# Ternary group means: ScalarE scales the sums out of PSUM into bfloat16, VectorE only applies the lower bound

## The reference

```python
def ternary_quant(w_fp32, g=64):
    w = w_fp32.astype(jnp.bfloat16)
    w_g = w.reshape(-1, g)
    scale = jnp.clip(jnp.mean(jnp.abs(w_g), axis=-1, keepdims=True), 1e-08, None)
    q = jnp.clip(jnp.round(w_g / scale), -1, 1)
    w_hat = (q * scale).reshape(w.shape)
    return w + jax.lax.stop_gradient(w_hat - w)
```

## Time and profile before

| | us |
|---|---|
| median of 3 runs | 684.52 |
| lowest and highest | 682.62, 688.56 |
| the profiled execution | 689.13 |
| its span, first to last instruction | 687.2 |
| TensorE busy | 569.5 |
| VectorE busy | 490.9 |
| ScalarE busy | 307.2 |
| GpSimd busy | 216.8 |

### The profile page before, as it was taken

One profiled execution on the slowest core, in us unless ns is written; L12 is line 12 of the kernel. 1 busy time (PEld: TensorE's weight loads), 2 busy tenths in 40 slices (PEclk: granted clock), 3 DMA queues, 4 the chain that ended last, 5 costly groups with the idle time before them and its releaser, 6 DMA issues.

```text
span 687.2 us, 10946 instructions
## 1 busy us (share of the span) xinstructions
PE 569.5 (83%) x3678; PEld 405.9 (59%) x3678; DVE 490.9 (71%) x1066; ACT 307.2 (45%) x563; POOL 216.8 (32%) x225
## 2 busy tenths in 40 slices
PE   2777699689577799998599988898978889999990
PEld 1544377468356688884355554464535478888870
DVE  5799966997895486868558678768871467777753
ACT  2749222223322233551456545545535656666640
POOL 2666556247544223674200010010044011121120
PEclk9999899899699899996789999999979999999995
DMA  6222000000320005499954331500025793000005
GB/s 183 85 82 88 1 0 1 1 0 17 87 63 16 1 1 174 90 207 259 199 89 80 71 70 26 95 2 2 2 76 231 277 372 123 23 24 32 24 31 191
DMA packets 32733, 58.36 MB, mean 85 GB/s; under 512 B 6822, under 2 KB 24646, under 8 KB 30118
## 3 DMA queue, kind: packets, MB, share of 16 engines
q1 hardware_dynamic: 30422, 52.32, 28.4%
q0 software_dynamic: 1872, 5.13, 2.1%
q10 hardware_dynamic: 384, 0.20, 0.1%
HBM read 41.84 MB, written 15.51 MB: 83 GB/s over the span
## 4 chain that ended last, share of the span: by engine, by line
PE 39%; DVE 9%; DMA 4%; ACT 3%; POOL 2%; issue 2%; SPq 1%; ACTq 0%; POOLq 0%; DVEq 0%
PE bank L826 19%; PE bank L1089 5%; PE bank L820 4%; PE bank L1066 4%; DVE small L1828 3%; PE bank L1039 3%; DMA Qs<-mT 2%; PE bank L1068 1%; PE bank L1041 1%; DMA pieces<-P 1%; SPq L721 1%; ACT PTa L1372 1%; DMA yt<-results 1%; PE bank L1106 1%; POOL P3c L2258 1%
## 5 line engine op out<-in xcount | busy, mean ns | idle before, releaser
L1828 DVE TENSOR_REDUCE small<-bank 128x1 f32<-128x256 f32 (+3 forms) x256 | 107.7, 483 | 15.1 <-PE bank L1041 14.1
L1039 PE MATMUL bank<-Ks,Qs 96*128 96x256 bf16 (+3 forms) x256 | 66.6, 328 | 8.5 <-DVE small L1828 7.1
L2094 DVE TENSOR_TENSOR wl<-wall,wh 128x1024 fp32r<-128x1024 f32 x46 | 56.2, 1222 | 22.2 <-ACT wh L1511 20.9
L1066 PE MATMUL bank<-Qs,Ks 99*128 99x512 bf16 (+3 forms) x256 | 60.4, 312 | 7.9 <-DMA Qs<-mT 5.6
L1372 ACT ACTIVATE PTb<-bank 128x512 f32<-128x512 f32 (+1 forms) x96 | 43.9, 529 | 34.9 <-PE bank L1068 34.4
L1372 ACT ACTIVATE PTa<-bank 128x512 f32<-128x512 f32 (+1 forms) x96 | 43.5, 529 | 33.8 <-PE bank L1068 28.9
L1066 PEld LDWEIGHTS bank<-Qs,Ks 99*128 99x128 bf16 x256 | 25.6, 100 | 51.4 <-issue 24.5
L1041 PE MATMUL bank<-maskb,identb 128*128 128x128 bf16 x256 | 55.3, 234 | 0.0
L1323 ACT ACTIVATE sg<-bank 128x512 f32<-128x512 f32 (+1 forms) x28 | 16.7, 598 | 75.9 <-PE bank L826 75.9
L1511 ACT CAST wh<-wall 128x1024 fp32r x46 | 48.0, 1044 | 1.8 <-issue 0.7
L1068 PE MATMUL bank<-identb,maskb 128*128 128x128 bf16 x256 | 48.2, 225 | 0.0
(11 more groups left out here) (362 smaller groups left out, 1531.2 us busy)
## 6 DMA issues: line engine op xcount, KB each, us to landing
wall<-e_pack SPq DMA_DIRECT2D x8, 1536.0 KB, 8.4
Qs<-pieces SPq DMA_DIRECT2D x48, 128.0 KB, 6.0
stg<-w_pack SPq DMA_DIRECT2D x18, 256.0 KB, 2.7
pieces<-P SPq DMA_DIRECT2D x9, 512.0 KB, 9.9
wf<-t_pack SPq DMA_DIRECT2D x12, 256.0 KB, 2.7
Ks<-pieces SPq DMA_DIRECT2D x8, 384.0 KB, 5.5
sorted_rows<-blank SPq DMA_DIRECT2D x1, 2944.0 KB, 12.1
Ks<-pieces SPq DMA_DIRECT2D x8, 256.0 KB, 5.7
```

What stands on the lines that cost most here:

```text
L1039: nc.tensor.matmul(banks[b][:, o:o + w], Q[0:96, h, i * P:(i + 1) * P], K[0:96, h, 0:w], start=True, stop=False)
L1066: nc.tensor.matmul(banks[b][:, o:o + w], K[0:99, h, j * P:(j + 1) * P], Q[0:99, h, j * P:CH], start=True, stop=False)
L1828: last = nc.vector.tensor_reduce(mxv[:, i, h:h + 1], banks[b][:, o:o + w], AX.X, ALU.max, negate=True)
L2094: nc.vector.tensor_tensor(weight_part("l", i, half), wall[:, bass.ds(place + half * KC * EI, KC * EI)], weight_part("h", i, half).bitcast( ...
```

## The change

The mean is split in two. A new function `group_mean` on ScalarE copies the sums from bank 3 with the scale 1/64 into `scl` (bfloat16), once per piece, and takes over the two waits for the former contents of `scl`. VectorE then applies only the lower bound, from `scl` to `scl` in SBUF ("the bound"), and waits for ScalarE instead of TensorE. TensorE may write bank 3 again when ScalarE has read it. Nothing else is moved; the new ScalarE instruction stands where the sums stand in the table of slots.

```diff
--- before.py
+++ after.py
@@ -326,6 +326,7 @@
         decay = tally("decay_ready")
         sgl = tally("silu_g_ready")
         t_abs = tally("ternary_abs")
+        t_mean = tally("ternary_mean")
         t_scl = tally("ternary_scale")
         t_sgn = tally("ternary_digits")
         t_over = tally("ternary_difference")
@@ -890,7 +891,7 @@
                 ab, scl, over = L0["ab"][:, i % 4, :], L0["scl"][:, i % 2, :], L0["over"][:, i % 2, :]
                 same_group, minus_half = L0["grp"][:, 0, :], L0["grp"][:, 1, :]
                 b = TERN_BANKS[stage]
-                claim(b, (t_scl, t_sgn, t_put)[stage], p)
+                claim(b, (t_mean, t_sgn, t_put)[stage], p)
                 if stage == 0:
                     pe.wait_ge(*t_abs.upto((p, 0)))
                     pe.wait_ge(*setup.upto("grp"))
@@ -1314,6 +1315,14 @@
                 nc.scalar.activation(L0["ab"][:, i % 4, :], L0["wf"][:, i % 2, :], ACT.Abs).then_inc(*t_abs.tick((p, 0)))
                 nc.scalar.activation(L0["sgn"][:, i % 4, :], L0["wf"][:, i % 2, :], ACT.Sign).then_inc(*t_abs.tick((p, 1)))
 
+            def group_mean(p):
+                i = PIECES.index(p)
+                act.wait_ge(*mm.upto(("tern", p, 0)))
+                if i >= 2:
+                    act.wait_ge(*t_over.upto(PIECES[i - 2]))
+                    act.wait_ge(*mm.upto(("tern", PIECES[i - 2], 1)))
+                nc.scalar.activation(L0["scl"][:, i % 2, :], banks[TERN_BANKS[0]][:], ACT.Copy, scale=1.0 / 64).then_inc(*t_mean.tick(p))
+
             def mlp_gate(s, gb):
                 (kind, c), m, n = steps[s]
                 M = SW[m] if kind == "sw" else P
@@ -1412,6 +1421,8 @@
                     nc.scalar.activation(v, v, ACT.Silu).then_inc(*sgl.tick((c, pr)))
                 elif op == "ternA":
                     absolute(it[1])
+                elif op == "tern" and it[2] == 0:
+                    group_mean(it[1])
                 elif op == "w" and it[1] in ("w1", "w3", "w2"):
 
                     if it[1] == "w2":
@@ -1635,13 +1646,12 @@
                 i = PIECES.index(p)
                 bank = banks[TERN_BANKS[stage]]
                 scl, digit = L0["scl"][:, i % 2, :], L0["tern"][:, i % 2, :]
+                if stage == 0:
+                    dve.wait_ge(*t_mean.upto(p))
+                    nc.vector.tensor_scalar(scl, scl, 1e-8, None, ALU.max).then_inc(*t_scl.tick(p))
+                    return
                 dve.wait_ge(*mm.upto(("tern", p, stage)))
-                if stage == 0:
-                    if i >= 2:
-                        dve.wait_ge(*t_over.upto(PIECES[i - 2]))
-                        dve.wait_ge(*mm.upto(("tern", PIECES[i - 2], 1)))
-                    nc.vector.tensor_scalar(scl, bank[:], 1.0 / 64, 1e-8, ALU.mult, ALU.max).then_inc(*t_scl.tick(p))
-                elif stage == 1:
+                if stage == 1:
                     dve.wait_ge(*t_abs.upto((p, 1)))
                     nc.vector.scalar_tensor_tensor(digit, bank[:], 0.0, L0["sgn"][:, i % 4, :], ALU.is_gt, ALU.mult)\
                         .then_inc(*t_sgn.tick(p))
```

## The result

The kernel after takes 695.05 us (median of 4 runs, 692.11 to 696.55), the kernel before 686.54 us (median of 4, 682.62 to 689.99; three of the four are the runs that the prediction stood on). The ratio is 1.0122 with a 95% interval of 1.0075 to 1.0170, which is 8.4 us longer (5.1 to 11.7). The forecast was 690.1 us, with 694.0 as the upper end. So the direction was right and the size too small. A loss of more than 1% had a chance of 0.28 in the prediction, and this is one.

The account below looks back on a forecast made before the run. The prediction took VectorE's repeating slot of work per weight piece to bound the kernel. Start 2.6, regular slots 2.5 and long slots 0.5 gave +5.6 us, on the median 684.52 a forecast of 690.1 us, range 685.0 to 694.0.

Parts of the forecast that it names:

- What bounds the kernel: Ternary weight stage, 30 to 87 us: whatever starts VectorE's next slot later, one slot per weight piece, makes the kernel longer.
- The start: First pieces: the first mean copy queues on ScalarE behind signs that wait for a DMA; +2.6 us, bounds 2.3 and 2.9.
- The longer way: Third piece at the start: sums, copy, bound take 0.87 us to VectorE's next instruction against 0.64 before, so 0.23.
- the clock: Rival, TensorE at the start and in slots: its clock stays low after the longer pause; +7.4, 691.9 us; chance 0.06.
- The price of the bound: VectorE's bound in SBUF takes 0.30 us instead of 0.69; 0.39 saved 12 times, 4.7 us the whole possible gain.
- What takes the gain: Seven regular slots: GpSimd's read-out holds the bound, which ends 0.15 us behind it; slots of 4.41 us, +2.5 us.
- The long slots: Two slots with the value rows: ScalarE's decay rows get behind the copy; bounds 0 and 1.0, taken as +0.5 us.
- (1): Rival, regular slots: the bound passes beside GpSimd unheld; the start remains, +2.3, 686.8 us; chance 0.20.
- (2): Rival, VectorE: its relief decides, all 4.7 us come through against the start's 2.6; -2.1, 682.4 us; chance 0.06.
- (3): Rival, VectorE's bound: it stays at one element a cycle, 0.39 more in seven slots; +8.3, 692.8 us; chance 0.10.
- (4): Rival, TensorE: its clock stays low after the longer pause, with products and sums slower; +7.4, 691.9 us; chance 0.06.

Follow-up runs that it names:

- e3: The whole change, but on ScalarE the first piece's mean copy stands ahead of the third piece's absolute values and signs; ratio 1.0034 to the kernel before.
- e7: The whole change, but in the first long slot ScalarE does decay rows, then mean copy, then values and signs; ratio 1.0110 to the kernel before.
- e4: The whole change, but the bound is a three-operand instruction that also reads the sums from PSUM; ratio 1.0118 to the kernel before.
- e5: The whole change, but ScalarE's copy adds 1e-8 as a bias and VectorE applies no bound; ratio 0.9971 to the kernel before.
- e9: The whole change with a bound also reading PSUM, and the first piece's copy ahead of the third's values and signs; ratio 1.0059 to the kernel before.

## Why the prediction was right and wrong

**What bounds the kernel: right.** What starts VectorE's next slot later made the kernel longer: the interval of each ratio holds the shift of the last split. That the two spans differ by 7.2 us as the last splits do (7.19) is partly luck, as what lies behind the last split scatters by 6.6 us.

**The start: the cause right, the size not, 3.54 instead of 2.6.** The queue behind the DMA was named, and e3, which changes only the place in it, takes the whole loss away. Three things were left out of the term. The first bound ended 2.66 late instead of 2.33, as the DMA came 0.22 later and the copy did not overlap the signs; the 0.22 belongs to this execution, and e7, whose start is the same, has 3.21 in all. The longer way was counted at the third piece only; the second piece paid 0.31 too. And the clock, which stood among the rivals at 0.06, was part of it: TensorE's pause was 5.05 us instead of 2.48, the granted clock in the start's stretch (30 to 42.4 us) 0.59 against 0.80 before (30 to 38.5), and products and sums took 1.43 instead of 1.17 us, 0.26 more. That the longer pause made the clock low was not tested. 2.66 + 0.31 + 0.26, and 0.31 for the third piece (0.23 forecast), are the 3.54. The bound of 2.9 on this term was too tight: it took a held bound as the only thing that could go wrong.

**The price of the bound: right.** 0.293 us free, 0.30 forecast.

**What takes the gain: right.** Slots of 4.42 to 4.45 against 4.41, +2.66 against +2.5. e4 shows the hold as what makes all seven slots alike, and e5 what a slot is without the bound. The averages agree, but not slot by slot: the slots of before take 3.51 to 4.38, and in the one of 3.51 some 0.5 of the loss of 0.94 would be there without a hold, by the longer way (e4, e9). What of the bound needs something that GpSimd holds, its reading, its writing or its form, was not taken apart.

**The long slots: 0.98 instead of 0.5.** The step considered only the decay rows behind the copy and took the middle of its bounds. It did not ask whether the bounds of the long slots are held as well. In the first (+0.60) the wait for the copy made the loss after the change, and in e7, without that wait, the hold made the same; the hold makes the second (+0.38).

**Rivals.** (1), the bound passing beside GpSimd, is out: in all seven regular slots it ended 0.15 or 0.16 us behind the read-out. (2) is out, as VectorE's busy time shows no relief. (3) is out, 0.29 us where GpSimd is idle. (4) did not decide, but it put 0.26 into the start; in the slots the read-out covered it, as the prediction said (0.95 of cover; the slot at a clock of 0.69 took 4.42).

**The range.** What failed is the size of two terms of the sum, the start (0.9 more) and the long slots (0.5 more). With the regular slots the terms come to 7.2 by the traces, 1.6 above the sum of 5.6. Of the 4.95 us by which the result lies above the forecast, 2.0 more are the base: the forecast stood on 684.52, the median of three, and a fourth run made it 686.54. The last 1.3 lie between the medians (8.5 us apart) and the traces (7.2), which these few runs don't resolve. The runs of before in later comparisons have medians of 685.1 to 687.9. The range took that base as exact and allowed the forecast's own terms 0.8 us above their sum, so its upper end was too near.

## What to carry to other kernels

Before work is handed to another engine, look at the head of that engine's queue: an instruction that waits for a DMA passes its wait to all behind it, and here one place in an order was worth 3.3 us. A scaling on VectorE whose operands all move into SBUF can lose its own speed where GpSimd is at work at that moment (here 0.95 to 1.11 us instead of 0.29 in half of the bounds): see what GpSimd does in the same 0.3 us before counting a saving. When a held instruction sets a slot, removing it can gain more than its duration (here 1.07 us for 0.29), and another change of the order may pay only then (the same edit gave nothing in the long slots with it and at least 1.4 us without).

## What the runs showed of the hardware

The held bound ends 0.15 us behind GpSimd's instruction in regular and long slots alike, whether that is a float32 read-out (60.05, 60.20) or a bfloat16 difference (64.95, 65.10), while an instruction of VectorE with a PSUM operand ran its 0.69 us inside a read-out. GpSimd's own instructions were hardly longer for it, 1200 against 1162 ns at the median for the difference. TensorE's granted clock falls below 0.95 in one regular slot of before and of after and in three of e4, and what a slot at some 0.7 costs differs: 0.3 us before (4.38 against 4.10), nothing after the change (4.42), 0.8 us in e4 (4.88 against 4.10).
